# A new common order of the 371 pieces of a layer, and PSUM rings that run on through the layers

## The reference, cut to what matters

```python
for i in range(NL):                      # NL = 6, H = 16 heads of HD = 8
    xn = _adaln(x, noise_emb, n1_w[i], n1_b[i])
    q, k, v = jnp.split(xn @ qkv_w[i].T, 3, axis=-1)      # rope on q and k
    x = x + _attn(q, k, v, src_mask).reshape(B, L, D) @ so_w[i].T
    xn = _adaln(x, noise_emb, n2_w[i], n2_b[i])
    q, k, v = rope(xn @ cq_w[i].T), rope(context @ ck_w[i].T), context @ cv_w[i].T
    x = x + _attn(q, k, v, ctx_mask).reshape(B, L, D) @ co_w[i].T
    xn = _adaln(x, noise_emb, n3_w[i], n3_b[i])
    h = jax.nn.gelu(xn @ f1_w[i].T + f1_b[i], approximate=False)
    x = x + (h @ f2_w[i].T + f2_b[i])
```

## Time and profile before

| what | us |
|---|---|
| median of 3 runs (3528.18 to 3543.38) | 3539.87 |
| the profiled execution | 3527.18 |
| its span, first to last instruction | 3525.4 |
| PE busy | 2973.8 (84%) |
| DVE busy | 2083.9 (59%) |
| ACT busy | 1909.4 (54%) |
| POOL busy | 806.0 (23%) |
| mean granted TensorE clock | 0.954 |

### The profile page before, as it was taken

The page is one execution under the profiler, slowest core; times in us unless marked ns, Lnnn a source line. Parts: engine busy times, 40 slices in busy tenths (PEclk is TensorE's granted clock), DMA queues, the critical chain, the costliest instruction groups (busy, mean ns, idle before and its releaser), DMA issues.

```text
span 3525.4 us, 44936 instructions
## 1 busy us (share of the span) xinstructions
PE 2973.8 (84%) x15735; PEld 1044.5 (30%) x15735; DVE 2083.9 (59%) x3631; ACT 1909.4 (54%) x2693; POOL 806.0 (23%) x1327
## 2 busy tenths in 40 slices
PE   7998999868888787888878856878888788888878
PEld 2563333222222222222222221222222222222226
DVE  4326777548375674746658266658375674746634
ACT  5432333337566574665657534647566574665642
POOL 0003454502212222212212102212212222212211
PEclk9999999879999999999999977999999999999999
DMA  1100000001110111101011001011110111101020
GB/s 42 55 17 8 1 1 1 11 21 41 33 37 27 41 29 32 43 22 52 21 35 41 22 9 45 23 34 41 35 37 27 39 31 32 43 22 51 19 96 36
DMA packets 125514, 110.11 MB, mean 31 GB/s; under 512 B 49982, under 2 KB 116076, under 8 KB 125292
## 3 DMA queue, kind: packets, MB, share of 16 engines
q1 hardware_dynamic: 114924, 97.80, 9.3%
q10 hardware_dynamic: 10368, 9.44, 0.9%
HBM read 41.96 MB, written 0.52 MB: 12 GB/s over the span
## 4 chain that ended last, share of the span: by engine, by line
PE 62%; DVE 20%; ACT 7%; POOL 5%; issue 4%; ACTq 1%; SPq 1%; DMA 1%; DVEq 0%; POOLq 0%
PE ps L524 11%; DVE arena L807 10%; PE ps L469 5%; PE ps L498 4%; PE ps L655 4%; PE ps L597 3%; ACT arena L680 3%; PE ps L640 3%; PE ps L553 2%; PE ps L541 2%; DVE arena L809 2%; PE ps L1501 2%; PE ps L583 2%; PE ps L1489 2%; PE ps L532 2%
## 5 line engine op out<-in xcount | busy, mean ns | idle before, releaser
L680 ACT ACTIVATE arena<-ps 128x1024 f32<-128x1024 f32 x960 | 936.4, 1024 | 348.1 <-PE ps L498 345.2
L807 DVE TENSOR_REDUCE arena<-ps 128x1 f32<-128x512 f32 x1536 | 963.8, 683 | 178.7 <-PE ps L469 167.1
L524 PE MATMUL ps<-arena 128*32 128x512 f32 x3840 | 513.1, 609 | 21.2 <-ACT arena L680 17.9
L469 PE MATMUL ps<-arena 49*128 49x512 bf16 x1536 | 308.4, 398 | 238.5 <-DVE arena L807 201.4
L498 PE MATMUL ps<-arena 52*128 52x512 bf16 x1920 | 344.1, 385 | 32.3 <-ACT arena L680 27.6
L809 DVE TENSOR_REDUCE arena<-ps 128x3 f32<-128x462 f32 (+1 forms) x576 | 303.0, 579 | 89.4 <-PE ps L476 82.7
L889 POOL TENSOR_TENSOR arena<-arena,zeros 128x16 bf16<-128x16 f32 x192 | 42.2, 220 | 1011.3 <-DVE arena L807 582.4
L469 PEld LDWEIGHTS ps<-arena 49*128 49x128 bf16 x1536 | 75.1, 93 | 567.4 <-DVE arena L807 472.7
L899 POOL TENSOR_TENSOR arena<-arena 128x512 f32<-128x512 f32 x96 | 121.9, 1270 | 450.2 <-ACT arena L712 450.2
L905 POOL TENSOR_TENSOR arena<-arena 128x512 bf16<-128x512 f32 (+1 forms) x84 | 92.5, 1101 | 549.2 <-ACT arena L739 549.2
L818 DVE TENSOR_TENSOR h<-ps,h 128x512 f32<-128x512 f32 x48 | 33.2, 691 | 293.0 <-PE ps L553 293.0
(11 more groups left out here) (383 smaller groups left out, 4350.9 us busy)
## 6 DMA issues: line engine op xcount, KB each, us to landing
arena<-arena SPq DMA_DIRECT2D x720, 64.0 KB
arena<-we_dram SPq DMA_DIRECT2D x24, 578.5 KB, 7.5
arena<-arena ACTq DMA_DIRECT2D x144, 64.0 KB
w<-weights_dram SPq DMA_DIRECT2D x26, 320.0 KB, 3.0
w<-weights_dram SPq DMA_DIRECT2D x13, 512.0 KB, 3.8
arena<-arena SPq DMA_DIRECT2D x384, 6.0 KB
arena<-arena SPq DMA_DIRECT2D x288, 19.2 KB
w<-weights_dram SPq DMA_DIRECT2D x39, 128.0 KB, 2.1
```

The lines of the kernel that those rows point to most:

```text
L469: pe.matmul(s_bank(slot + r), qst[b][rows, idx, P * qt:P * (qt + 1)], kst[b][rows, idx, :], start=True, stop=True).then_inc(s_full, 1 + (z ...
L524: mm = pe.matmul(bank(7)[32 * j:32 * j + 32, :], v, prob[:, slot, j, :], start=(g % 2 == 0 and kt == 0), stop=(a == 0 and g % 2 == 1 and k ...
L680: act.activation(prob[:, chunk_no(b, a, g, kt) % NPROB, 2 * p:2 * p + 2, :], e_bank(slot).rearrange("p (j n) -> p j n", j=2), ACT.Exp, sca ...
L807: op = ve.tensor_reduce(nmax[:, g % 2, r, n:n + 1], s_bank(slot + r), AX.X, ALU.max, negate=True)
```

## The change

Two things change. `PLACES` gets new numbers for nearly all pieces, and the rings' counts no longer start at a padding at each walk: bank and wait follow the running count, and each `then_inc` raises by 1. Functions, durations and shapes of the instructions are not edited, nor is `FILL`. The diff, cut (the other `then_inc` edits are alike):

```diff
 PLACES = {
-    ('turn', 0, 0): [17, 35, 66, 102],
+    ('turn', 0, 0): [16, 40, 70, 97],
-    ('turn', 1, 0): [137, 159, 190, 220],
+    ('turn', 1, 0): [125, 150, 179, 213],
-    ('exp', 1, 0): [[[147, 151, 156, 167], [149, 152, 161, 168]], [[172, 178, 185, 193], [173, 182, 192, 196]],
-        [[205, 211, 218, 224], [208, 212, 223, 228]], [[234, 238, 245, 249], [235, 239, 246, 254]]],
+    ('exp', 1, 0): [[[137, 153, 158, 162], [138, 154, 160, 166]], [[169, 176, 186, 191], [174, 181, 190, 193]],
+        [[197, 201, 206, 215], [198, 203, 207, 220]], [[222, 229, 236, 240], [223, 230, 238, 243]]],
...
-    ('evac', 0): [[90, 133], [279, 291]],
-    ('evac', 1): [[200, 259], [344, 367]],
-    ('sel', 0): [[92, 138], [283, 292]],
-    ('sel', 1): [[206, 264], [349, 368]],
-    ('inv', 0): [[93, 144], [284, 293]],
-    ('inv', 1): [[210, 265], [352, 369]],
-    ('out',): [[145, 298], [271, 370]],
-    ('center',): [[-45, 157, 302], [38, 285, 373]],
-    ('var',): [[-35, 163, 303], [45, 288, 376]],
-    ('apply',): [[-33, 169, 304], [46, 294, 379]],
+    ('evac', 0): [[92, 141], [270, 284]],
+    ('evac', 1): [[210, 253], [350, 361]],
+    ('sel', 0): [[144, 148], [286, 288]],
+    ('sel', 1): [[217, 263], [362, 364]],
+    ('inv', 0): [[147, 151], [287, 290]],
+    ('inv', 1): [[262, 264], [363, 365]],
+    ('out',): [[159, 294], [274, 366]],
+    ('center',): [[-50, 164, 295], [23, 278, 369]],
+    ('var',): [[-47, 168, 298], [27, 281, 372]],
+    ('apply',): [[-43, 170, 299], [34, 285, 374]],
...
-    ('f1',): [[306, 308], [382, 384]],
-    ('f2',): [316, 393],
+    ('f1',): [[302, 306], [384, 379]],
+    ('f2',): [313, 388],
...
 }
...
-            for ring, size in RING.items():
-                if ring in more and count[ring] == 0:
-                    total = sum(steps(i).get(ring, 0) for i, _ in order)
-                    count[ring] = -total % size
...
     def use(self, ring, item):
-        n = self.done[self.place[item]][ring] - steps(item)[ring]
-        return n % RING[ring], self.began(ring) + n
+        n = self.began(ring) + self.done[self.place[item]][ring] - steps(item)[ring]
+        return n % RING[ring], n

     def room(self, ring, item, uses):
-        return floor0(self.use(ring, item)[1] - max(RING[ring] - uses, self.skipped(ring, item)))
+        return max(self.use(ring, item)[1] - (RING[ring] - uses), 0)
...
-                                  start=True, stop=True).then_inc(s_full, 1 + (z.skipped("s", it) if r == 0 else 0))
+                                  start=True, stop=True).then_inc(s_full, 1)
```

More of the change, by code:

```diff
@@ L86 @@
 PLACES = {
[L87 to L92, removed]
@@ L134 @@
[L134 to L137 removed]
+    ('score', 0, 0): [[-3, -1, 0, 2, 6, 9, 10, 11], [14, 15, 20, 22, 24, 26, 28, 32], [38, 42, 46, 52, 54, 56,
+        60, 63], [67, 69, 72, 76, 80, 83, 86, 89]],
+    ('score', 0, 1): [[208, 211, 216], [219, 224, 227], [231, 237, 247], [250, 256, 258]],
+    ('score', 1, 0): [[94, 96, 102, 104, 107, 110, 112, 116], [119, 122, 124, 129, 132, 136, 139, 142], [146,
+        149, 155, 157, 161, 163, 165, 167], [175, 182, 187, 189, 192, 196, 200, 205]],
@@ new lines @@
+    ('score', 1, 1): [[301, 303, 304], [305, 307, 312], [318, 320, 322], [323, 325, 332]],
+    ('msplit', 0, 0): [12, 33, 64, 90],
+    ('msplit', 0, 1): [218, 228, 248, 259],
+    ('msplit', 1, 0): [117, 145, 178, 212],
+    ('msplit', 1, 1): [309, 314, 329, 336],
+    ('turn', 0, 0): [16, 40, 70, 97],
+    ('turn', 0, 1): [233, 235, 254, 265],
+    ('turn', 1, 0): [125, 150, 179, 213],
+    ('turn', 1, 1): [310, 315, 330, 337],
+    ('mrow', 0, 0): [18, 49, 78, 98],
+    ('mrow', 0, 1): [234, 242, 255, 266],
@@ new lines @@
+    ('mrow', 1, 0): [131, 152, 180, 214],
+    ('mrow', 1, 1): [311, 326, 339, 340],
+    ('exp', 0, 0): [[[19, 25, 31, 43], [21, 30, 37, 44]], [[51, 58, 65, 71], [53, 59, 66, 75]], [[81, 87, 95,
+        101], [82, 88, 100, 103]], [[108, 114, 120, 126], [109, 115, 121, 128]]],
+    ('exp', 0, 1): [[[245], [246]], [[251], [260]], [[272], [273]], [[275], [276]]],
+    ('exp', 1, 0): [[[137, 153, 158, 162], [138, 154, 160, 166]], [[169, 176, 186, 191], [174, 181, 190, 193]],
+        [[197, 201, 206, 215], [198, 203, 207, 220]], [[222, 229, 236, 240], [223, 230, 238, 243]]],
@@ new lines @@
+    ('exp', 1, 1): [[[317], [319]], [[333], [334]], [[342], [343]], [[347], [348]]],
+    ('pv', 0, 0): [[35, 36, 47, 55], [62, 68, 85, 91], [105, 111, 113, 118], [123, 130, 135, 140]],
+    ('pv', 0, 1): [[261], [267], [277], [280]],
+    ('pv', 1, 0): [[156, 172, 173, 188], [194, 199, 202, 209], [221, 225, 232, 239], [241, 244, 249, 252]],
+    ('pv', 1, 1): [[331], [344], [355], [357]],
+    ('tail',): [[257, 279], [327, 353]],
+    ('pvt',): [[[268, 269], [282, 283]], [[345, 349], [359, 360]]],
@@ L138 @@
+    ('ktail',): 226,
+    ('vals',): [7, 79, 185],
+    ('f1',): [[302, 306], [384, 379]],
+    ('f2',): [313, 388],
+    ('gain',): [-75, 4, 297],
+    ('biasf',): 127,
+    ('load',): {'cout': 477, 'cross': 410, 'ffn': 642, 'n0': -63, 'n1': 5, 'n2': 400, 'self': 316, 'sout': 470},
 }
@@ L213, in began @@
     def began(self, name):
-        return self.start[name] + self.turn * self.total[name]
+        return self.start[name]
     def has(self, item, asker):
@@ L597, in proj @@
                     pe.matmul(s_bank(slot + i)[:, 0:B * CTX if u == 3 else S], w[:, base + P * i:base + P * (i + 1)], src,
-                              start=True, stop=True).then_inc(s_full, 1 + (z.skipped("s", it) if i == 0 else 0))
+                              start=True, stop=True).then_inc(s_full, 1)
             def vals(it):
@@ L705, in sel @@
                 act.wait_ge(den_inv, z.ahead("inv", it))
-                act.activation(rlog, e_bank(slot)[:, 0:S], ACT.Ln).then_inc(e_free, 1 + z.skipped("e", it))
+                act.activation(rlog, e_bank(slot)[:, 0:S], ACT.Ln).then_inc(e_free, 1)
             def inv(it):
@@ L718, in center_h @@
                 act.activation(cols(sq, b), e_bank(slot)[:, 0:S], ACT.Square).then_inc(squared, 1)
-                act.activation(cols(centered, b), e_bank(slot)[:, 0:S], ACT.Copy).then_inc(e_free, 1 + z.skipped("e", it))
+                act.activation(cols(centered, b), e_bank(slot)[:, 0:S], ACT.Copy).then_inc(e_free, 1)
             def var(it):
@@ L754, in vals @@
                     act.activation(dst[:, :, 0, :, 0:HD], src[:, :, 0], ACT.Copy)
-                    act.activation(dst[:, :, 1, :, 16:16 + HD], src[:, :, 1], ACT.Copy).then_inc(e_free, 1 + z.skipped("e", it))
+                    act.activation(dst[:, :, 1, :, 16:16 + HD], src[:, :, 1], ACT.Copy).then_inc(e_free, 1)
                     return
@@ L1542, in turn2 @@
                 act.wait_ge(e_full, at + 1)
-                act.activation(nmrow2[0:35, u % 2, :], e_bank(slot)[0:35, 0:S], ACT.Copy).then_inc(e_free, 1 + z.skipped("e", it))
+                act.activation(nmrow2[0:35, u % 2, :], e_bank(slot)[0:35, 0:S], ACT.Copy).then_inc(e_free, 1)
             def wide2(it):
@@ L1550, in wide2 @@
                 act.wait_ge(e_full, at + 1)
-                act.activation(nmwide2[:, u % 2, :], e_bank(slot), ACT.Copy).then_inc(e_free, 1 + z.skipped("e", it))
+                act.activation(nmwide2[:, u % 2, :], e_bank(slot), ACT.Copy).then_inc(e_free, 1)
             def exp2(it):
@@ L1576, in den2 @@
                 act.wait_ge(e_full, at + 1)
-                act.activation(dlog2, e_bank(slot)[:, 0:S], ACT.Ln).then_inc(e_free, 1 + z.skipped("e", it))
+                act.activation(dlog2, e_bank(slot)[:, 0:S], ACT.Ln).then_inc(e_free, 1)
                 act.wait_ge(e_free, at + 1)
```

103 lines of the change are left out of this document (38 added, 65 removed), and 6 rows, old and new, of the table PLACES.

## The result

| | before | after |
|---|---|---|
| median, us | 3541.62 (4 runs, 3528.18 to 3546.79) | 3644.82 (4 runs, 3633.29 to 3647.39) |
| profiled execution, us | 3527.18 | 3646.03 |
| first stack, us | 1315.5 | 1367.9 |
| mean granted clock | 0.954 | 0.937 |

The changed kernel takes 1.0313 times as long [1.0297, 1.0329]: 103 us more by the medians, where +97 and 3636 us were forecast.

A forecast was written before the change was run, and what follows sets the result against it. PE was taken as the bound, its idle time a matter of order. Exposed table loads of +168 us and the order's -71 us made +97 us on 3539.9, a median of 3636 us; range 3528 to 3750, the forecast's own 3580 to 3710.

The forecast's parts named there:

- The loads: Turned `f1` halves add 222 ACT table loads of 1.283 us, 22 in each of 10 walks; 16.8 us exposed a walk, +168 us.
- Rival 1: The missing set at `f1` costs only two loads a walk, hidden in ACT's idle time; 3469 us, chance 0.07.
- rival 2: Loads in the walks' `sel`, `inv` and `var` mostly hidden, a third of the exposure: 3525 us, chance 0.10.
- rival 4: A table switch costs ACT the load's own time again, 285 us more: 3921 us, chance 0.02.
- The chains: Places in a walk where PE waits for ACT's added loads, summing to 16.8 us of the 28.2 us of loads.
- something else is in the range and not in the sum: Granted clock falls to 0.50 where PE idled; one or two more dips in 10 walks, +17 to +34 us.
- rival 3: All added loads in the walks exposed and the order gives nothing: 3822 us, chance 0.10.
- scores: Score pairs too close on PE: waits fall from 21.0 to 16.3 us, -4.7 us in each walk.
- `sel` and `pv`: At the ends of the attentions, moved `sel` and `exp` remove PE waits: -3.6 us a walk.
- `exp` with `mrow`: From `turn` to a group's first `exp`, four groups fall short by 4.4 us: +2.4 us a walk, bounds 0 and 4.4.
- 1.2 us apart: Two scores less than 1.2 us of PE work apart make PE wait the rest; 16.3 us in the new order.
- The rings: Removing the padding at walk seams moves the wait to `center`: 0, bounds -0.9 and +0.3 us a seam.

The follow-up runs named there:

- 4, rings alone: Kernel before the change, with only the padding of the ring counts at a walk's start removed, its old order kept: 3532.58 us, ratio 1.0002.
- 8, ends moved: Kernel before the change, with only the ends of the two cross attentions set as in the new order: 3548.37 us, ratio 1.0044.
- 5, order alone: Kernel before the change, with the new order, halves of `f1` in order, and its old ring padding kept: 3399.88 us, ratio 0.9625.
- 1, halves in order: Changed kernel with the two `f1` halves of batch element 1 turned back into order (379, 384): 3354.35 us, ratio 0.9486 to the kernel before.
- 2, sets by order: Changed kernel, order untouched, Gelu set named ahead of whichever `f1` half comes first, common set behind the other: 3360.03 us, ratio 0.9506 to the kernel before.
- 7, late turn: Experiment 1's kernel with `turn` and `mrow` of one group moved 8 places later, towards its `exp`: 3436.35 us, ratio 0.9732 to the kernel before.
- 9, shadow: Experiment 1's kernel with both table sets named once more behind half 1 of `f1`, 4 loads more a walk: 3444.78 us, ratio 0.9761.
- 10, norms: Experiment 1's kernel with the pair of table sets switched in each `var`, 12 loads more a walk: 3488.26 us, ratio 0.9879.
- 3, old order, turned: Kernel before the change, old order, with only the two `f1` halves of batch element 1 exchanged (384, 382): 3868.34 us, ratio 1.0936.
- experiment 6: Experiment 1's kernel with `FILL = {}`, the discarded matmuls left out: 3412.86 us, ratio 0.9671 to the kernel before.
- experiment 11: Experiment 5's kernel with one more discarded fill matmul ahead of `out (1, 1)`: 3396.59 us, ratio 0.963 to the kernel before.

## Why the prediction was right, and where it was not

**What a walk consists of.** Means over the four middle walks of the first stack, in one profiled execution of each kernel, us; "low" is the time at a granted clock of 0.50, loads are those added.

| kernel | walk | PE idle | low | loads |
|---|---|---|---|---|
| before | 212.4 | 33.8 | 12.8 | 0 |
| 4, rings alone | 212.3 | 32.1 | 17.1 | 0 |
| 8, ends moved | 213.3 | 32.6 | 18.8 | 0 |
| 5, order alone | 202.1 | 21.8 | 18.9 | 0 |
| 1, halves in order | 196.1 | 21.1 | 6.0 | 0 |
| 2, sets by order | 196.0 | 21.0 | 6.0 | 0 |
| 7, late turn | 201.3 | 24.5 | 11.1 | 0 |
| 9, shadow | 202.9 | 24.5 | 14.5 | 4 |
| 10, norms | 207.1 | 27.6 | 14.5 | 12 |
| after | 222.8 | 39.5 | 22.2 | 22 |
| 3, old order, turned | 245.6 | 49.9 | 49.5 | 22 |

In each row the walk less its idle time less half of the low time is between 170.9 and 172.3 us: PE's work at full clock (162 us in experiment 6, without the fill). Two quantities, idle and low, account for the walks of all these kernels. But the idle time alone does not tell the low time: experiments 4, 5 and 8 have less idle time than the kernel before, and more low time.

**The loads.** Kind and place were right, and the number nearly: 224 more for the forecast 222, 26 in each of ten walks, and in each `post` walk 4 for 2 where I had counted 3, because the common set is loaded once more behind the last half. ACT is busy 2190.0 us for the forecast 2194. A walk takes 223 us, as forecast, but by luck (below). Rival 1 (two loads only) is refuted by the count, rival 2 (hidden) by experiment 2, rival 4 (a switch costs as long again) by the timeline, where an activation starts 0.01 us behind its load. The chains, after less experiment 2, same order, idle time of PE in us a walk:

| chain | forecast | measured |
|---|---|---|
| `sel`, `inv` (0, 0), the `exp` behind | 3.5 | 3.1 |
| `var (0, 1)` | 1.9 | 2.3 |
| `sel (1, 0, 0)` | 2.1 | 1.9 |
| `sel`, `inv` (1, 0, 1), `out (1, 0)` | 1.4 | 2.0 |
| `var (1, 1)`, four of (0, 1), `out (0, 1)` | 4.3 | 5.3 |
| `var (0, 2)`, `f1 (0, 0)` | 1.6 | 1.6 |
| `var (1, 0)` | 2.0 | 2.7 |
| sum | 16.8 | 18.9 |

The idle time as a whole rose by 18.5 us. The working chain by chain holds. What failed is the sentence that set the clock aside, "something else is in the range and not in the sum": PE is also busy 8.2 us a walk longer, at the low clock. The loads cost not 16.8 but some 27 us a walk. In the second stack it is more. The four middle walks there, of the kernel after and of experiment 2:
```profile
2387.03:3296.63 909.60, 750.58 (x4121) 228.39 (x4122) 525.30 (x889) 629.47 (x797) 195.31 (x380) 0.93 0.11 32
```
```profile
2248.66:3027.07 778.41, 694.62 (x4120) 216.71 (x4120) 526.43 (x889) 518.63 (x709) 195.00 (x380) 0.99 0.13 37
```
A walk is 32.8 us longer there, 18.8 of it idle and 14.0 busy. In all, the loads cost 285 us against experiment 2 and 290 against experiment 1, and not 168. The size is that of rival 3, the loads at their full ACT time (282 us); but it is the sum of partial exposure and of clock, not full exposure.

**The order.** Forecast -5.9 us a walk (bounds -10 and 0), -71 in all; measured -16.3 us a walk and -174 us (experiment 1, with the rings), outside the bounds. Idle time by kind of piece, before less experiment 1: scores -8.2 (forecast -4.7), `sel` and `pv` -4.3 (forecast -3.6), `exp` with `mrow` +0.1 (forecast +2.4), the rest near 0, -12.7 together; and -3.5 of busy time by the clock. So three things: the rule "1.2 us apart" overstated the waits that stay in the new order, 16.3 us for 13.9 measured; the `mrow` chain was taken as 4.6 us and is 3.75, and in experiment 1 the four groups in question have between 3.6 and 4.9 us for it; the clock again. Rival 3's half, that the order gives nothing, is refuted.

**The rings.** Right in the old order (1.0002), wrong in the new one, where the padding costs 45 us (the bounds allowed some 13): a walk is 6.0 us longer, and half of the added low time is 6.4 us. Most of that low time stands at the seams. Of the -16.3 us some 6 are the rings'. That the wait of 0.7 us is what lowers the clock there is not shown; fill (experiment 11) did not undo it, and a kernel with the padding and a shorter wait at the seam was not tried.

**The sum.** +168 - 71 = +97 us was forecast. The parts are +290 and -174, together +116: 3644.82 less the 3528.64 us of the kernel before that ran beside experiment 1. Against the 3541.62 us that it took beside the changed kernel it is +103. Direction and mechanism are shown. That the forecast of 3636 us lies 9 us off is luck: the first part was too small by 122 us, the second by 103 us, and the two nearly cancel. The clock that was left out is nearly all of the first (8.2 us in each middle walk of the first stack, 14.0 in the second, in 10 walks) and some 40% of the second (3.5 us in each of 12); the rest of the second is idle time that I sized too small.

## What to carry to other kernels

When an order is planned by a program, the state that handlers set for each other (here: the first half names a function table, the second restores it) is a constraint of the order; count the table loads of the new order before timing it, and bind the naming to what comes first and last. In a kernel bound by PE, price a wait at more than its length: in nearly every edit here that added idle time, PE's busy time grew too, at a lower granted clock. Measure a walk as work at full clock plus idle plus half of the low time. And test the parts of a change separately: here one line hid a gain of 5% behind a loss of nearly 9%.

## What the runs showed that I had not expected

- Taking 8.6 us of useless matmuls out of a walk made it 5.6 us longer (experiment 6).
- The price of a table load of 1.283 us was between 0.9 us (experiment 10) and 1.7 us (experiment 9) of a walk in the first stack, depending on where it stood and on the clock.
- A wait longer by 0.7 us stood ahead of 10 us at half clock (experiment 5).
